# The middle stage of a two-layer transformer kernel as a wave of four batches, with another form of the scan

## The chip, the cores and the metric

The kernel runs on one core of a Trainium2 chip. The core has a matrix engine (PE, TensorE; its weight loads are counted apart as PEld), three engines for element-wise work (DVE or VectorE, ACT or ScalarE, POOL or GpSimd) and a queue for transfers (SP, SyncE). Each runs its own instructions in the order in which they are written, and they wait for each other through semaphores. The metric is the time of one execution on the device, in microseconds.

## The reference

The input is 4 x 1024 tokens of 128 features. Two layers are computed, each with an attention of 16 heads of 8 features and a second part, and each followed by a layer norm over the features (`ln` below; the norms outside have no gain or bias):

```python
# layer 0, attention part (inner residual block)
attn = causal_attention(ln(x) * g + b) @ out_w + out_b      # q, k, v by 128x128 weights
xs, vs = ln(x + attn) * g1 + b1, 0
for _ in range(8):                                            # the scan
    u  = tanh(attn @ w_ctx + xs @ w_x + b_inl)
    vs = vs + 0.1 * (u - xs - vs)
    xs = xs + 0.1 * vs
y = x + attn + xs
y = y + gelu((ln(y) * g2 + b2) @ ff_w1 + ff_b1) @ ff_w2 + ff_b2      # 128 -> 512 -> 128
x = ln(x + y)
# layer 0, second part: a linear layer plus a low-rank term
x = ln(x + x @ weight.T + pooled(x) @ disha)
# layer 1: full attention, then relu feed-forward
x = ln(x + full_attention(x) @ Wout + bout)
x = ln(x + relu(x @ W1 + b1) @ W2 + b2)
```

## The kernel before, in words

The kernel has five stages, one behind the other, each a block of its own that ends with all engines meeting: `first_stage` (norm and q, k, v of layer 0), `attention` (causal), `middle_stage`, `attention` (full), `last_stage`. Activations stay on the chip in `x_tm`, `v_tm` and `attn_tm` (tokens on partitions, 32 tiles of 128 tokens). q and k are cut into three bf16 parts, written to DRAM and loaded again per group of heads in the order that the attention wants. The attention stages follow a list of entries written out ahead (`attention_order`), with no loops left in them.

The edit is in the middle stage. It holds everything between the two attentions: the output projection of attention 0 (L889), the norm before the scan, the scan, the norm before the feed-forward, the feed-forward (L932 up, L921 down), two norms with the linear layer between them, and q, k and v of layer 1 (`Qkv`, L552 and L521).

It runs as a hardware loop of two turns (`Fori(0, NLOOP)`). One turn takes 2048 tokens as four chunks of 512; each chunk has one or two of the eight PSUM banks. On every engine the order is step by step: all four chunks of one step, then all four of the next. Features lie on partitions in most steps, so data are turned between steps by PE against an identity matrix (`turn`, L514).

The scan keeps two tensors, `xs` and a scaled velocity `w`, and the product in PSUM is never formed anew: at its start the bank gets the context term and the x term (L899, L900), and each further step adds `wx_step` times `w` (L908), which is what the change of `xs` contributes. A step of one chunk is: ACT's tanh from PSUM (L802), POOL's `u - xs` (L761), DVE's new `w` (L850), PE's addition (L908), and DVE's new `xs` (L853):

```python
pool.tensor_tensor((t if k else w)[:, c, :], u[:, c, :], xs[:, c, :], ALU.subtract)
dve.scalar_tensor_tensor(out=w, in0=w, scalar=1.0 - DT, in1=t, op0=ALU.mult, op1=ALU.add)
dve.scalar_tensor_tensor(out=xs, in0=w, scalar=DT * DT, in1=xs, op0=ALU.mult, op1=ALU.add)
pe.matmul(bank[c], wx_step, w[:, c, :], start=False, stop=True)
```

`Norm` makes statistics per tile on DVE (L472, L477), the inverse root on POOL (L504, L507: an addition and a power over the four columns of a chunk), and applies it on DVE (L484). POOL also makes the residual with a bias (L751, L766). `Qkv` brings q and k out of PSUM into fp32 with a bias (L566), makes the first bf16 part on ACT (L573), the rest on DVE for q and on POOL for k (L585), the second part on ACT (L578), and the third on DVE or POOL (L589); SP writes each chunk (L604, 384 KB a transfer) and loads the first three groups of heads for the next attention ahead. The attention's own SP program waits for the writes of all chunks.

Ahead of the stage stands a small block on DVE that scales `w_x` once (L1200) and adds the two linear weights (L1202).

Of the kernel before, what the change touches and what calls it, by code (L numbers as in the profile page):

```python
# [4 lines left out]
F32 = mybir.dt.float32  # L5
# [5 lines left out]
P = 128  # L11
# [4 lines left out]
DT = 0.1  # L16
# [26 lines left out]
FREE = 1  # L43

# [122 lines left out]
def attention(nc, taken, name, causal, scr, scr_m, slots, loaded, written, v_tm, attn_tm, ident, mask2, id2, ident_bf):  # L167
# [27 lines left out]
    with ExitStack() as ctx:  # L195
# [29 lines left out]
        def _(sp):  # L225
# [10 lines left out]
            for c in range(NCH):  # L236
                sp.wait_ge(written[c], 2 * 16 * NLOOP + FREE)
# [457 lines left out]
def middle_stage(nc, taken, W, C, R, scr, slots, loaded, written, x_tm, v_tm, attn_tm, ident, roots,  # L695
                 wx_step, w_lin):


    with ExitStack() as ctx:
        def sb(n, shape=(P, NCH, CH), dt=F32):  # L700
            return ctx.enter_context(nc.sbuf_tensor(f"m_{n}", list(shape), dt))
# [3 lines left out]


        pool3 = ctx.enter_context(nc.sbuf_tensor("m_n_x2_xx", [P, 3, NCH, CH], F32))
        n_tm = pool3[:, 0, :, :]
        x2 = y2p = pool3[:, 1, :, :]
        xx = pool3[:, 2, :, :]  # L710
        parts = pool3[:, :, :, :].rearrange("p a c t -> p (a c t)").bitcast(BF16)
        parts = parts.rearrange("p (s c j t) -> p s c j t", s=2, c=NCH, j=PARTS)
        part = [parts[:, s, :, :, :] for s in range(2)]
        both = ctx.enter_context(nc.sbuf_tensor("m_u_t", [P, 2, NCH, CH], F32))
        at = u = both[:, 0, :, :]
        aT = t = both[:, 1, :, :]
        hh = [both[:, i, :, :] for i in range(2)]
        cT = hT = sb("cT_hT")
        x1 = x3 = sb("x1_x3")
        xs = y1 = sb("xs_y1")  # L720
        w = y2 = sb("w_y2")
        bank = banks(ctx.enter_context(nc.psum_tensor("m_ps", [P, 8 * BANK], F32)))
        ln1, ln2, ln3, ln4 = (Norm(ctx, nc, taken, f"m_ln{i}", roots) for i in range(1, 5))
        qkv = Qkv(ctx, nc, taken, "m_qkv", W("q1"), W("k1"), W("v1"), C("bq1"), C("bk1"), R("bv1"),
                  scr, slots, loaded, written, v_tm, (hh[0], hh[1]), part)
        (at_ready, at_turned, aT_ready, c_mm, cT_ready, c_turned, x1_ready, n1_turned, xs_ready, z_ready,
         tanhed, lagged, sped, moved, xs_turned, xb_ready, x2_ready, xx_ready, n2_turned, hT_ready, f_mm, gelued,
         o_mm, x3_ready, y1_turned, y1T_ready, lin_mm, y2p_ready, y2_turned, y2T_ready, y2_kept) = (sem(n) for n in (
             "at_ready at_turned aT_ready c_mm cT_ready c_turned x1_ready n1_turned xs_ready z_ready tanhed lagged "
             "sped moved xs_turned xb_ready x2_ready xx_ready n2_turned hT_ready f_mm gelued o_mm x3_ready y1_turned "  # L730
             "y1T_ready lin_mm y2p_ready y2_turned y2T_ready y2_kept").split())
        block = ctx.enter_context(nc.Block())

        @block.sync
        def _(sp):
            qkv.on_sync(sp)

        @block.gpsimd
        def _(pool):
            pool.sem_inc(qkv.parted[1], FREE)  # L740
            with pool.Fori(0, NLOOP) as it:
                n0 = NCH * it
                for c in range(NCH):
                    ln1.root(pool, n0 + c, c)

                for c in range(NCH):

                    for i in range(NCH):
                        if c == 0:
                            pool.wait_ge(written[i], FREE + 2 * 16 * it)  # L750
                    pool.tensor_tensor(rows(xx[:, c, :]), x_tm[:, chunk_tiles(it, c), :],  # L751
                                       R("fb2").unsqueeze(1).to_broadcast([P, CT, P]), ALU.add)\
                        .then_inc(xb_ready, 1)
                for k in range(ITERS):
                    for c in range(NCH):
                        m = (ITERS * it + k) * NCH + c
                        pool.wait_ge(tanhed, m + 1)
                        if k:

                            pool.wait_ge(moved, m - NCH + 1)  # L760
                        pool.tensor_tensor((t if k else w)[:, c, :], u[:, c, :], xs[:, c, :], ALU.subtract)\  # L761
                            .then_inc(lagged, 1)
                for c in range(NCH):
                    pool.wait_ge(x2_ready, n0 + c + 1)
                    pool.wait_ge(xb_ready, n0 + c + 1)
                    pool.tensor_tensor(xx[:, c, :], xx[:, c, :], x2[:, c, :], ALU.add).then_inc(xx_ready, 1)  # L766
                for c in range(NCH):
                    ln2.root(pool, n0 + c, c)
                for c in range(NCH):
                    ln3.root(pool, n0 + c, c)  # L770
                for c in range(NCH):
                    ln4.root(pool, n0 + c, c)
                qkv.rest(pool, 1, it)
# [488 lines left out]
```

## Time and profile before

| | |
|---|---|
| median of 3 runs | 1732.08 us (1728.84 to 1732.10) |
| profiled execution | 1729.09 us |
| its span, from the first to the last instruction | 1727.2 us |
| PE, PEld busy | 1436.7 us (83%), 588.4 us (34%) |
| DVE busy | 1345.7 us (78%) |
| ACT busy | 1074.1 us (62%) |
| POOL busy | 403.6 us (23%) |
| mean granted TensorE clock | 0.900 of full |
| moved by DMA | 47.82 MB |

An engine is busy while one of its instructions runs; waits are not counted. Matmuls overlap, so the busy time of PE says that it had work, not how well it was used. The granted clock is a mean over a stretch in parts of the full 2.4 GHz; at any instant it is one of two levels. A matmul of fp32 data shows as two records. In order of time the first stage ends near 88 us, the first attention near 538, the middle stage near 933 and the second attention before the last stage.

### The profile page before, as it was taken

What the parts mean: (1) busy time and instruction counts of PE and PEld (TensorE: products, weight loads), DVE (VectorE), ACT (ScalarE), POOL (GpSimd) and SP (SyncE); (2) the same over time, 40 slices, a digit from 0 to 9 for tenths busy, and PEclk for the clock granted to TensorE, in tenths of its full rate; (3) what the DMA queues carried; (4) which work ended last, traced back from release to release, by engine and by line L of the source; (5) the groups of instructions that cost most, each with busy time, mean ns of one, the idle gap of its engine ahead of it and who ended that gap; (6) DMA issues with size and microseconds to landing.
All of it is one profiled execution on the core that took longest, in us unless ns stands there. A gap on an engine that the chain in (4) does not pass through costs nothing. (4 is left out here: it accounts for less than half of the span.)

```text
span 1727.2 us, 33152 instructions
## 1 busy us (share of the span) xinstructions
PE 1436.7 (83%) x13008; PEld 588.4 (34%) x13008; DVE 1345.7 (78%) x1923; ACT 1074.1 (62%) x1287; POOL 403.6 (23%) x674
## 2 busy tenths in 40 slices
PE   3379999999996667567674899999999999999767
PEld 2234344333433225431351232323333323333455
DVE  3688888888872793649656999999999999996363
ACT  3527777777775323432323588888888888888422
POOL 1512232222321762356423000000000000000331
PEclk9659999999998768776686799999999999999888
DMA  3510110101000000030002000000110000000000
GB/s 102 165 57 21 40 40 22 41 22 40 22 3 2 0 0 1 10 119 0 0 0 73 20 21 21 21 21 21 28 31 22 21 21 21 3 2 3 1 25 24
DMA packets 45456, 47.82 MB, mean 28 GB/s; under 512 B 11392, under 2 KB 32768, under 8 KB 45184
## 3 DMA queue, kind: packets, MB, share of 16 engines
q1 hardware_dynamic: 44880, 45.32, 9.0%
q8 instruction: 97, 1.59, 0.4%
q10 hardware_dynamic: 432, 0.53, 0.1%
q14 instruction: 47, 0.39, 0.1%
HBM read 30.22 MB, written 15.47 MB: 26 GB/s over the span
## 5 line engine op out<-in xcount | busy, mean ns | idle before, releaser
L338 DVE TENSOR_REDUCE l_negp<-l_ps 128x2 f32<-128x1024 f32 (+2 forms) x832 | 951.9, 1180 | 74.1 <-PE l_ps L394 35.7
L308 ACT ACTIVATE l_pT<-l_ps 128x1024 f32<-128x1024 f32 (+1 forms) x832 | 819.8, 992 | 200.3 <-PE l_ps L410 171.3
L431 PE MATMUL l_ps<-l_pT,l_vs 128*32 128x256 f32 (+3 forms) x6640 | 512.3, 384 | 2.1 <-POOL l_pT L275 1.5
L388 PE MATMUL l_ps<-Ks,Qs 48*128 48x512 bf16 (+3 forms) x1792 | 335.0, 374 | 67.6 <-DVE l_negp L338 23.9
L410 PE MATMUL l_ps<-Qs,Ks 51*128 51x512 bf16 (+3 forms) x1792 | 319.7, 365 | 15.5 <-DVE l_negp L338 8.8
L431 PEld LDWEIGHTS l_ps<-l_pT,l_vs 128*32 128x32 f32 x6640 | 134.4, 108 | 167.6 <-issue 137.9
L410 PEld LDWEIGHTS l_ps<-Qs,Ks 51*128 51x128 bf16 x1792 | 81.2, 93 | 315.8 <-issue 148.0
L388 PEld LDWEIGHTS l_ps<-Ks,Qs 48*128 48x128 bf16 x1792 | 88.4, 94 | 227.5 <-ACT l_pT L308 91.3
L275 POOL TENSOR_SCALAR_AFFINE_SELECT l_pT<-l_pT 128x512 f32<-128x512 f32 x128 | 81.1, 635 | 302.4 <-ACT l_pT L308 302.4
L908 PE MATMUL m_ps<-m_w_y,wx_step 128*128 128x512 f32 x112 | 88.8, 915 | 35.8 <-DVE m_w_y L850 35.8
L262 POOL CAST l_parts<-l_negm 128x16 bf16<-128x16 f32 x64 | 12.6, 196 | 430.5 <-DVE l_negm L343 427.4
L802 ACT ACTIVATE m_u_t<-m_ps,c_sb 128x512 f32<-128x512 f32 x64 | 44.0, 687 | 97.1 <-PE m_ps L908 85.8
L761 POOL TENSOR_TENSOR m_u_t<-m_u_t,m_xs_y 128x512 f32<-128x512 f32 x56 | 88.8, 1600 | 35.5 <-ACT m_u_t L802 20.1
L853 DVE SCALAR_TENSOR_TENSOR m_xs_y<-m_w_y,m_xs_y 128x512 f32<-128x512 f32 x64 | 75.8, 1185 | 22.0 <-POOL m_w_y L761 20.0
L394 PE MATMUL l_ps<-mask,id 64*128 64x128 bf16 x1024 | 69.6, 224 | 0.0
L850 DVE SCALAR_TENSOR_TENSOR m_w_y<-m_w_y,m_u_t 128x512 f32<-128x512 f32 x56 | 62.8, 1121 | 0.0
L322 ACT ACTIVATE l_msp<-l_ps 48x128 bf16<-48x128 bf16 x64 | 17.3, 270 | 71.0 <-PE l_ps L441 70.9
L351 DVE RECIPROCAL l_rc<-l_ps 128x16 f32<-128x16 f32 x64 | 16.5, 257 | 56.5 <-PE l_ps L448 56.5
L253 POOL COPY l_vs<-v_tm 128x256 f32<-128x256 f32 x32 | 12.7, 397 | 198.9 <-PE l_ps L431 198.8
L908 PEld LDWEIGHTS m_ps<-m_w_y,wx_step 128*128 128x128 f32 x112 | 25.1, 265 | 97.7 <-DVE m_w_y L850 91.6
L394 PEld LDWEIGHTS l_ps<-mask,id 64*128 64x128 bf16 x1024 | 50.6, 99 | 21.0 <-issue 2.3
L514 PE MATMUL m_ps<-ident,m_n_x_xx 128*128 128x128 f32 x64 | 17.8, 434 | 40.5 <-DVE m_n_x_xx L484 40.5
(139 smaller groups left out, 1241.6 us busy)
## 6 DMA issues: line engine op xcount, KB each, us to landing
Qs<-scr_q SPq DMA_DIRECT2D x128, 64.0 KB
Ks<-scr_k SPq DMA_DIRECT2D x64, 96.0 KB
Qs<-scr_q SPq DMA_DIRECT2D x128, 32.0 KB
Ks<-scr_k SPq DMA_DIRECT2D x64, 64.0 KB
scr_q<-a_part SPq DMA_DIRECT2D x8, 384.0 KB, 3.7
scr_k<-a_part SPq DMA_DIRECT2D x8, 384.0 KB, 3.9
scr_q<-m_n_x_xx SPq DMA_DIRECT2D x8, 384.0 KB, 4.2
scr_k<-m_n_x_xx SPq DMA_DIRECT2D x8, 384.0 KB, 4.2
```

Of the source, the lines that this page charges most:

```text
L275: pool.affine_select(out=blk, in_=blk, compare_op=ALU.is_ge, fill=0.0, base=0, pattern=[[0, GH], [1, P]], channel_multiplier=-1).then_inc( ...
L308: act.activation(dst, src, ACT.Exp, scale=SCALE).then_inc(exped, 1)
L338: dve.tensor_reduce(dst, src, AX_X, ALU.max, negate=True).then_inc(reduced, 1)
L388: last = pe.matmul(outs[par], Qs[s][r:r + MROW, h2, qt * P:(qt + 1) * P], Ks[s][r:r + MROW, h2, at:at + w], start=True, stop=True)
L394: last = pe.matmul(outs[par][:, w - P:w], id2[r:r + ROWS, j, :], mask2[r:r + ROWS, j, :], start=False, stop=True, skip_group_check=True)
L410: last = pe.matmul(to[:, par, i * w:(i + 1) * w], Ks[s][r:r + MROW + 3, h2, kt * P:(kt + 1) * P], Qs[s][r:r + MROW + 3, h2, qh * CH + lo:( ...
L431: last = pe.matmul(pv_ps[q % 2][32 * h:32 * h + 32, a:a + wide], vs[g % 2][:, kt, h, :], pT[m % PRING][:, h, a:a + wide], start=n == first ...
L761: pool.tensor_tensor((t if k else w)[:, c, :], u[:, c, :], xs[:, c, :], ALU.subtract)\
L802: act.activation(u[:, c, :], bank[c], ACT.Tanh, bias=C("b_inl")).then_inc(tanhed, 1)
L850: dve.scalar_tensor_tensor(out=w[:, c, :], in0=w[:, c, :], scalar=1.0 - DT, in1=t[:, c, :], op0=ALU.mult, op1=ALU.add).then_inc(sped, 1)
L853: dve.scalar_tensor_tensor(out=xs[:, c, :], in0=w[:, c, :], scalar=DT * DT, in1=xs[:, c, :], op0=ALU.mult, op1=ALU.add).then_inc(moved, 1)
L908: pe.matmul(bank[c], wx_step, w[:, c, :], start=False, stop=True, skip_group_check=True)\
```

## The change

The signatures carry `written_all`, so that the attention waits for as much as the stage before it wrote. The middle stage is rewritten without a loop. Its unit is a batch of 1024 tokens with two PSUM banks of its own from the first step to the last, and all engines walk through one list, in which batch b is five steps behind batch b - 1:

```diff
+def wave(steps, lag):
+    order = [(i + lag * b, b, name) for i, name in enumerate(steps) for b in range(B)]
+    return [(name, b) for _, b, name in sorted(order)]
...
+    steps = (["turn_attn", "out", "turn_out", "scale1", "turn1", "ctx"] + [("scan", k) for k in range(ITERS)]
+             + ["turn_xs", "scale2", "turn2"] + [("up", j) for j in range(4)] + [("down", i) for i in range(4)]
+             + ["scale3", "turn3", "lin", "scale4", "turn4", "q", "k", "v"])
+    order = wave(steps, LAG)
```

One entry of the list is one step of one batch: a name that each engine looks up for its own share. `batch_mm` is two matmuls of 512 columns, `turn_batch` eight transposes, `batch_tokens_out` eight matmuls of 128 columns; `RowNorm` does statistics, root and scaling for eight tiles at once.

The scan keeps `x` alone, at two neighbouring steps in a ring of two buffers. Velocity is eliminated: x(k+1) is a combination of x(k), x(k-1) and the tanh, and a factor `BETA`, the root of 1 - 0.1, per step makes the coefficient of x(k-1) minus one. The factors go into scaled copies of `w_x`, one per step. In each step the context term is multiplied anew, and then the x term is added to it:

```diff
+                elif name[0] == "scan":
+                    k = name[1]
+                    now, then = ring[b][k % 2], ring[b][(k + 1) % 2]
+                    dve.wait_ge(tanhed[b % 2], ITERS * (b // 2) + k + 1)
+                    dve.wait_ge(lagged[b % 2], ITERS * (b // 2) + k + 1)
+                    dve.scalar_tensor_tensor(out=then, in0=u[b], scalar=DT * DT / BETA ** (k + 1), in1=then,
+                                             op0=ALU.mult, op1=ALU.add).then_inc(moved[b % 2], 1)
+                    if k < ITERS - 1:
+                        dve.wait_ge(moved[b % 2], ITERS * (b // 2) + k + 1)
+                        dve.scalar_tensor_tensor(out=now, in0=then, scalar=(2.0 - DT - DT * DT) / BETA, in1=now,
+                                                 op0=ALU.mult, op1=ALU.subtract).then_inc(lagged[b % 2], 1)
...
+                elif name[0] == "scan":
+                    k = name[1]
+                    if k:
+                        pe.wait_ge(tanhed[b % 2], ITERS * (b // 2) + k)
+                        batch_mm(pe, bank[b], W("ctx"), cT[b])
+                        pe.wait_ge(moved[b % 2], ITERS * (b // 2) + k)
+                    batch_mm(pe, bank[b], wx_of[k], ring[b][k % 2], start=False).then_inc(z_ready[b % 2], 1)
```

Further: the transposes of the attention's output read `attn_tm` itself; the identity is added to the linear weight, so that the residual comes out of the matmul and the fourth norm reads PSUM (`ln4.stats(dve, b, bank[b])`) and writes `x_tm` directly; POOL does only the two residual adds and the roots; the feed-forward's four hidden tensors lie in the scan's ring, `x1` and the norm's buffer; q and k go from PSUM straight to their first bf16 part on ACT, the rest and the third part on DVE. Gelu of one batch and tanh of later ones share ticks of the order. SP writes each batch in two transfers and waits for them before the stage ends:

```diff
+            for name, b in order:
+                if name == "v":
+                    for s in range(2):
+                        sp.wait_ge(s_parted[s], b + 1)
+                        dst = scr[s][:, :, b * SEQ:(b + 1) * SEQ]
+                        sp.dma_start(dst.rearrange("(j d) h t -> (d h) j t", d=HD), parts[:, b, s, :, :])\
+                            .then_inc(written[b], 16)
+                    if b == 0:
+                        sp.wait_ge(written[0], 32)
+                        for g in range(NG - 1):
+                            load_group(sp, scr, slots, loaded, g)
+            for b in range(B):
+                sp.wait_ge(written[b], 32)
...
+                for k in range(1, ITERS):
+                    dve.tensor_scalar(wx[:, k - 1, :], W("x"), BETA ** k, None, ALU.mult)
+                dve.tensor_tensor(w_lin[:, :], W("lin"), W("dis"), ALU.add).then_inc(lin_added, 1)
+                dve.wait_ge(lin_added, 1)
+                dve.tensor_tensor(w_lin[:, :], w_lin[:, :], ident[:, :], ALU.add)
```

## Rows read from the trace of the kernel before

**Rows 1.** The page: span, and busy time of the engines.
```profile
span 1727.2 us, 33152 instructions
PE 1436.7 (83%) x13008; PEld 588.4 (34%) x13008; DVE 1345.7 (78%) x1923; ACT 1074.1 (62%) x1287; POOL 403.6 (23%) x674
```

**Rows 2.** Order of time at the stage's ends: start us, us, engine line op, idle before.
```profile
541.23 0.23 DVE L1200 TENSOR_SCALAR wx_step<-w_sb 128x128 f32<-128x128 f32 x1 [3.00 <-PEq L115]
...
932.25 1.13 SPq L604 DMA_DIRECT2D scr_k<-m_n_x_xx  x1
...
933.83 0.61 PE L388 MATMUL l_ps<-Ks,Qs 48*128 48x512 bf16 x2 [15.71 <-PEq L699]
```

**Rows 3.** Busy us of PE, PEld, DVE, ACT, POOL (and count) by stretch; clock, DMA share, GB/s.
```profile
538.00:571.00 33.00, 14.99 (x59) 10.46 (x60) 15.78 (x55) 11.59 (x17) 9.77 (x12) 0.70 0.00 1
571.00:638.00 67.00, 49.26 (x69) 14.85 (x68) 59.55 (x52) 21.21 (x31) 47.87 (x30) 0.73 0.00 0
660.00:694.00 34.00, 30.57 (x165) 21.32 (x163) 8.74 (x39) 13.42 (x19) 3.09 (x6) 0.95 0.00 1
694.00:734.30 40.30, 23.88 (x108) 17.15 (x108) 25.70 (x78) 20.73 (x36) 14.70 (x17) 0.76 0.03 10
734.30:931.00 196.70, 130.54 (x432) 70.51 (x432) 128.15 (x280) 69.81 (x106) 92.47 (x83) 0.73 0.11 33
```

**Rows 4.** Who waited for whom in the middle stage: us in total, times, longest.
```profile
PEld m_ps L908 <- DVE m_w_y L850: 91.6, 48, 3.1
ACT m_u_t L802 <- PE m_ps L908: 85.8, 56, 3.6
```

**Rows 5.** Order of time in the scan, DVE and POOL.
```profile
628.94 0.68 DVE L850 SCALAR_TENSOR_TENSOR m_w_y<-m_w_y,m_u_t 128x512 f32<-128x512 f32 x1
629.03 5.05 POOL L761 TENSOR_TENSOR m_u_t<-m_u_t,m_xs_y 128x512 f32<-128x512 f32 x3 [0.56 <-DVE m_xs_y L853]
...
631.21 1.75 DVE L850 SCALAR_TENSOR_TENSOR m_w_y<-m_w_y,m_u_t 128x512 f32<-128x512 f32 x1
```

**Rows 6.** Order of time on PE, four stretches without a wait inside.
```profile
544.59 3.41 PE L514 MATMUL m_ps<-ident,m_u_t 128*128 128x128 f32 x16 [6.97 <-ACT m_u_t L784]
...
551.27 1.91 PE L514 MATMUL m_ps<-ident,m_cT_hT 128*128 128x128 f32 x16
...
668.59 3.73 PE L921 MATMUL m_ps<-w_sb,m_u_t 128*128 128x128 f32 x32
...
672.16 3.60 PE L932 MATMUL m_ps<-m_cT_hT,w_sb 128*128 128x512 f32 x8
```

**Rows 7.** ACT: order of time at the first gelu; then L308, ns min/median/max.
```profile
660.06 0.78 ACT L805 ACTIVATE m_cT_hT<-m_ps,c_sb 128x512 f32<-128x512 f32 x1 [0.51 <-PE m_ps L514]
...
660.85 1.28 ACT L813 ACT_TABLE_LOAD   x1
...
662.15 0.69 ACT L813 ACTIVATE m_u_t<-m_ps,c_sb 128x512 f32<-128x512 f32 x1
...
L308 ACT ACTIVATE l_pT<-l_ps x832: 592/1023/1138, 114.2 to 1604.9; 128x1024 f32<-128x1024 f32 x151, 128x512 f32<-128x512 f32 x16
```

**Rows 8.** Order of time in the norms; then L338, ns min/median/max.
```profile
556.55 0.36 DVE L477 BATCH_NORM_AGGREGATE m_ln_mv<-m_ln_bst 128x2 f32<-128x6 f32 x4
...
557.27 1.01 POOL L507 TENSOR_TENSOR m_ln_rs<-m_ln_ve,neg_half 128x4 f32<-128x4 f32 x1
...
646.19 0.87 DVE L472 BATCH_NORM_STATS2 m_ln_bst<-m_n_x_xx 128x6 f32<-128x128 f32 x4
646.23 1.26 POOL L766 TENSOR_TENSOR m_n_x_xx<-m_n_x_xx 128x512 f32<-128x512 f32 x1 [4.62 <-DVE m_n_x_xx L857]
...
653.61 1.11 DVE L484 TENSOR_SCALAR m_n_x_xx<-m_n_x_xx,m_ln_mv,m_ln_rs 128x128 f32<-128x128 f32 x4 [1.52 <-POOL m_ln_rs L507]
...
L338 DVE TENSOR_REDUCE l_negp<-l_ps x832: 679/1218/1228, 89.5 to 1580.3; 128x2 f32<-128x1024 f32 x135, 128x4 f32<-128x512 f32 x16, 128x2 f32<-128x768 f32 x16
```

**Rows 9.** L604, the writes of q and k: issue to landing.
```profile
DMA to landing us min/median/max: 2.5/4.1/6.2
```

More of the change, by code:

```diff
@@ L43 @@
 FREE = 1
+LAG = 5
 def part_runs(order):
@@ new lines, in turn_batch, with batch_mm, batch_tokens_out @@
+def turn_batch(pe, bank, src, ident):
+    for t in range(QT):
+        last = pe.transpose(bank[:, t * P:(t + 1) * P], src[:, t * P:(t + 1) * P], ident)
+    return last
+def batch_mm(pe, bank, weight, src, start=True):
+    for i in range(QH):
+        last = pe.matmul(bank[:, i * CH:(i + 1) * CH], weight, src[:, i * CH:(i + 1) * CH], start=start, stop=True,
+                         skip_group_check=not start)
+    return last
+def batch_tokens_out(pe, bank, src, weight):
+    for t in range(QT):
+        last = pe.matmul(bank[:, t * P:(t + 1) * P], src[:, t * P:(t + 1) * P], weight, start=True, stop=True)
+    return last
@@ L712, in middle_stage @@
[L712 to L731, printed above, removed]
+        three = sb("three", (P, B, 3, SEQ))
@@ L732, in middle_stage @@
+        f_mm, gelued = sem("f_mm"), sem("gelued")
+        assert LAG >= 4 and 2 * LAG >= ITERS
+        z_ready, tanhed, moved, lagged = (
+            [sem(f"{n}{i}") for i in range(2)] for n in "z_ready tanhed moved lagged".split())
+        s_mm, s_first, s_rest, s_second, s_parted = (
+            [sem(f"{s}_{n}") for s in "qk"] for n in "mm first rest second parted".split())
         block = ctx.enter_context(nc.Block())
@@ L738, in _ @@
+            for b in range(B):
+                sp.wait_ge(written[b], 32)
         @block.gpsimd
         def _(pool):
[L740 to L773, printed above, removed]
@@ new lines, in _ @@
+            for name, b in order:
+                if name == "turn_attn":
+                    pool.tensor_tensor(rows(xx[b]), rows(xs_tm[b]), R("fb2").unsqueeze(1).to_broadcast([P, QT, P]),
+                                       ALU.add).then_inc(xb_ready, 1)
+                elif name == "turn_out":
+                    ln1.root(pool, b)
+                elif name == "turn_xs":
+                    ln2.root(pool, b)
+                    pool.wait_ge(x2_ready, b + 1)
+                    pool.wait_ge(xb_ready, b + 1)
+                    pool.tensor_tensor(xx[b], xx[b], x1[b], ALU.add).then_inc(xx_ready, 1)
+                elif name == ("down", 3):
+                    ln3.root(pool, b)
+                elif name == "lin":
+                    ln4.root(pool, b)
```

371 lines of the change are left out of this document (204 added, 167 removed).

## The prediction

> **What bounds the kernel now.** I read the page, then busy time by stretch, then the waits of the middle stage, then the order of time inside it. The page gives 1727.2 us of span in an execution of 1729.09 us [rows 1]; the shown median, 1732.08, lies 3.0 above. The edit rewrites only the middle stage, and the two attention stages, the first and the last stage keep their work. So the question is what lies between 541.23, where the small block of weights ahead of the stage begins, and 933.83, the first matmul of the second attention [rows 2]: 392.6 us.
>
> In that stretch no engine is full. The second of the two like loop turns is 196.7 us long with PE busy 130.5, DVE 128.2, ACT 69.8, POOL 92.5, at a granted clock of 0.73 [rows 3], a mix of TensorE's two levels, 1.2 and 2.4 GHz. It is a chain with little beside it. In the scan (571 to 638) DVE is busy 59.6 of 67 us and PE 49.3, at 0.73; in the up and down matmuls (660 to 694) PE is busy 30.6 of 34 at 0.95; in layer norm, linear and QKV (694 to 734) PE 23.9 of 40.3 at 0.76. The waits agree: of the stage's waits, PE's weight loads wait 91.6 us for DVE's `w`, ACT's tanh 85.8 us for PE [rows 4]. And DVE is full there only because POOL is: a scalar_tensor_tensor of 512 columns takes 0.69 us while POOL rests and 1.75 us while POOL subtracts [rows 5]. The stage ends on waits, and a denser order can win time.
>
> **Cost of the pieces, for 1024 tokens.** PE, at full clock: eight records of L932 (four 512-column matmuls) take 3.60 us, so a pair takes 1.71; 32 records (16 small matmuls) of L921 3.73, so eight take 1.86; 16 transposes 1.91 (3.41 at the low level), so eight take 0.92 [rows 6]. ACT: 0.59 us at 512 columns and 1.02 at 1024 without a bias, 0.69 with a bias at 512; so 1.12 with a bias, 1.21 with a scale too [rows 7]. DVE: 0.68 us at 512 columns and 1.22 at 1024 [rows 8], so 1.22 for an add, as a lone scan operation's 0.68 [rows 5] agrees with at 512, and two dependent operations of the scan 2.4; statistics (0.87 and 0.36 for four tiles, issued closer than they last) 2.3 for eight; a scale 2.1 (1.11 for four); POOL's root, 1.01 for four columns and not shown for eight, between 1.0 and 2.0: I take 2.0, since the addition beside it costs 0.2 on as many columns and so the cost sits in the power itself; with the addition and gaps 2.5 [rows 8].
>
> **What goes and what comes.** Gone: 64 POOL subtractions, half of DVE's columns under contention, the copy of attention into `at`, eight x_tm copies, the adds before the fourth norm. The scan keeps two scalar_tensor_tensor a step, and the first alone stands before the next matmul; POOL is idle in it, so I price them uncontended. POOL's eight adds of 1024 columns (about 2.5 us each from 1.26 at 512 [rows 8]) can hold DVE for up to 1.1 us each at the contended price; at DVE's 186 us in some 300 that is covered, and uncovered it is 8 x 1.1 = 9 us. Added: per step and batch another ctx matmul. Before, the scan had 8 x 9 = 72 matmuls of 512 columns; now it has 4 x 8 x 4 = 128: 56 x 0.855 = 48 us more PE work at full clock. PE's sum per batch: 23 pairs (39.3), six groups of eight small ones (11.2) and seven groups of eight transposes (6.4), so 57 and 228 us for four. DVE's is 15 scan operations at 1.2 (18.0), three adds with statistics (10.5), lin's statistics (2.3), four scales (8.9), the start of the scan (0.7, between half and all of 1.2), q, k and v (6.0): 46.4, so 186.
>
> **The order.** 33 steps a batch, five apart, make 48 ticks. Within a tick I take the largest of PE's sum, DVE's sum and the longest single step. PE by step: transposes 0.92; out, ctx, the first scan step, each up, q and k 1.71; the other seven scan steps 3.42; each down, lin and v 1.86; the scales none. Single steps: a scan step is tanh 1.12, two pairs 3.42 (the ctx pair covers DVE's 1.22) and gaps, 4.8; the first 4.2; turn_out and turn_xs 6.9; the last down 7.9; lin 6.7; up 3.0; q and k 4.4; scales 2.3 (the fourth, which reads PSUM and which no row shows, 2.8, my estimate, bounds 2.3 and 3.3); v 3.3; other transposes 2.2 to 2.4; out 3.0. The ticks:
> 0 to 9: 2.2 3.0 6.9 2.3 2.4 2.6 4.2 6.9 4.8 4.8, together 40.1;
> 10 to 29: 6.0 6.8 8.3 6.8 6.9 6.0 7.8 9.5 8.6 7.0 6.8 7.9 10.4 10.4 9.4 6.6 7.1 8.8 7.0 7.9, together 156.2 (PE's own sum 148.5);
> 30 to 47: 5.4 5.4 7.3 3.6 7.9 4.4 4.5 6.7 2.8 7.9 4.4 4.4 6.7 2.8 2.2 4.4 4.4 3.3, together 88.5.
> Tick 22, as an example, holds down 1 of batch 0, up 0 of batch 1 and a scan step of batches 2 and 3: 1.86 + 1.71 + 3.42 + 3.42 = 10.4 on PE, beside 4.8 of DVE. Sum 284.8.
>
> At 148 of 156 us PE is as dense as in 660 to 694, so the full clock holds there. In ticks 33 to 47 PE has 40.5 of 70 us, the share of 694 to 734; at that clock, 0.76, it adds 40.5 x 0.316 = 13; the first five, 4.5 us of PE at the 0.70 of 538 to 571 [rows 3], add 2. That makes 300 us.
>
> ACT changes function set wherever a gelu and a tanh share a tick: 17 to 20, 22 to 25, 27 and 28, two loads each, and one at 29: 21 loads of 1.28 us [rows 7], 27 us on ACT. Its worst tick becomes 3.4 + 2.6 = 6.0 beside 9.5 of PE: covered. In the trace the load begins 0.01 us behind the activation before it ends and the gelu starts 1.30 after the load began [rows 7]; I price a switch at 1.3.
>
> The Trainium skill (ScalarE: Activation LUTs, "What ACT_TABLE_LOAD costs") gives a switch some 2.66 us, load and drain, and tells authors to do all calls of one set together, which this wave undoes. By it the 21 switches are 56 us; the trace does not show the drain.
>
> **Both ends of the stage.** Ahead: seven more small operations on DVE at 0.23 [rows 2], the dependent add, then a barrier: 3.0 us from 541.23. Behind: SP now waits for each batch's writes inside the stage. Landing took 4.1 us in the median and 6.2 at most for 384 KB [rows 9], now 768 KB; the last `v` (3.3) covers part: 5 us, bounds 0 and 10. Unrolling puts loops' code into a straight line; I price that at nothing, as the attention's is such.
>
> Sum: 1729.1 - 392.6 + 3.0 + 300 + 5 = 1644.5; at the median's level 1647.
>
> **Rivals.**
> (a) Queues hold each other: every engine runs strictly in the written order, so each of 16 scales that waits 2.5 us for POOL's root holds the scan operations queued behind it on DVE. If all show on PE: 16 x 2.5 = 40 us, 1687. For: DVE's sum passes PE's in ticks 12, 14, 24. Against: a whole tick of other batches' work lies between statistics and scale.
> (b) The function sets end on the path: gelu holds the tanh of the scan. 27 us: 1674; for it, ticks 19, 20, 24, 25 have one or two scans and little cover; against it ACT's low share. At the skill's price it would be 1703.
> (c) Slower: PE becomes the bound at the low clock. The new stage rests on PE; the scan before ran at 0.73. With PE's terms divided by the clock the ticks give 354 us at 0.73 (1701), 389 at 0.65, and 490 at the lowest level throughout (1837). It turns slower below about 0.66. For: 32 batch steps with waits in them. Against: the dense ticks look like 660 to 694.
> (d) Better packing: chains of neighbouring ticks overlap, which my maximum per tick forbids. Ticks 0 to 9 of batch 0 alone (40), PE's 148, and the last batch's steps from tick 30 (58) give 246, some 50 less: 1593 at the very best; a third of it is 1628.
> That the change does not thin the scan's DVE work would show as (a).
>
> **Chances.** Forecast 0.58, (a) 0.15, (b) 0.08, (c) 0.08, three parts in four of it slower, (d) 0.11. The range is 1618 to 1692: it leaves out most of (c) and the far ends of (a) and (d). A difference of 0.2% is about what can be told from none here. Faster 0.93, same 0.01, slower 0.06.
>
> **What would show it.** PE over 85% busy at a clock above 0.9 in ticks 16 to 24; scan operations on DVE near 1.2 us, not 1.7; 21 or so table loads; the stage about 308 us from the weights block to the attention's first matmul. PE waits for DVE of more than 40 us in all would show (a), waits for gelu and tanh (b), a clock under 0.8 (c). Any change in the attention stages' time would make the sum wrong.

## The result, and the profile after

| | before | after |
|---|---|---|
| median | 1731.24 us (1728.84 to 1732.10, four executions) | 1658.05 us (1655.79 to 1660.02, four executions) |
| ratio, with its 95% interval | | 0.9579 [0.9561, 0.9597] |
| profiled execution, span | 1729.09, 1727.2 us | 1656.61, 1654.9 us |
| mean granted clock | 0.900 | 0.935 |

The change is faster by 73 us; the forecast had 84 (1647), and the range held it. The page of the kernel after answers to [rows 1]: POOL's busy time falls by 123 us, DVE's by 55 and ACT's by 41, while that of PE, the busiest, hardly moves (1436.7 to 1432.2): the span falls because PE waits less. PE has more matmuls than before and runs them at a higher clock.

```profile
span 1654.9 us, 32470 instructions
PE 1432.2 (87%) x13120; PEld 596.0 (36%) x13120; DVE 1290.7 (78%) x1850; ACT 1032.7 (62%) x1164; POOL 280.6 (17%) x554
```

The order of time at the ends of the middle stage, kernel after (start us, us, engine, line, operation, idle before), answers to [rows 2]:

```profile
542.72 1.04 DVE L1268 TENSOR_SCALAR wx<-w_sb 128x128 f32<-128x128 f32 x7 [3.00 <-PEq L116]
544.59 1.94 PE L742 MATMUL m_ps<-ident,attn_tm 128*128 128x128 f32 x8 [5.49 <-PEq L1261]
...
858.01 1.22 DVE L947 TENSOR_TENSOR v_tm<-m_ps,r_sb 128x1024 f32<-128x1024 f32 x1 [1.19 <-PE m_ps L757]
861.69 0.61 PE L389 MATMUL l_ps<-Ks,Qs 48*128 48x512 bf16 x2 [3.72 <-PEq L776]
```

From 542.72 to 861.69 are 319.0 us, against 392.6 before and 308 in the forecast. What lies behind the stage is unchanged (1654.9 - 861.69 = 793.2, before 1727.2 - 933.83 = 793.4); what lies ahead is 1.5 us longer. So the profiled execution is 12.1 above the forecast's 1644.5, of which 11.0 are in the stage: ahead 1.9 us (forecast 3.0), the ticks from 544.59 to the last `v` at 859.23 314.6 (forecast 300), behind 2.5 (forecast 5).

Busy us of PE, PEld, DVE, ACT, POOL (and count) by stretch, then clock, DMA share and GB/s, kernel after. The stretches are the whole stage, then the ticks 0 to 9, 10 to 29 and 30 to 47 with the end; they answer to [rows 3]:

```profile
542.70:862.00 319.30, 254.01 (x978) 147.99 (x980) 201.26 (x491) 97.63 (x89) 57.85 (x41) 0.89 0.08 28
542.70:595.60 52.90, 30.78 (x88) 16.12 (x89) 26.09 (x68) 9.94 (x9) 12.54 (x7) 0.73 0.00 1
595.60:763.60 168.00, 155.01 (x542) 84.09 (x541) 113.80 (x237) 57.60 (x52) 29.76 (x18) 0.96 0.00 0
763.60:861.70 98.10, 67.91 (x352) 47.66 (x351) 61.27 (x186) 30.09 (x29) 15.25 (x16) 0.86 0.25 89
```

In the dense middle PE is busy 155 of 168 us at a clock of 0.96. Measured against the forecast, ticks 0 to 9 took 51.0 us (42.1 with the clock's 2), 10 to 29 168.0 (156.2), 30 to 47 95.6 (101.5 with the clock's 13).

Who waited for whom in the stage (us in total, times, longest), kernel after, answers to [rows 4]. `PE` is the matmul itself, `PEld` the load of its weights:

```profile
ACT m_three L863 <- PE m_ps L749: 80.2, 32, 4.3
PE m_ps L742 <- DVE m_three L734: 27.4, 8, 9.9
PE m_ps L742 <- DVE x_tm L734: 11.0, 3, 7.2
...
PEld m_ps L749 <- DVE m_three L905: 6.2, 5, 2.6
...
PE m_ps L749 <- DVE m_three L905: 2.6, 3, 1.8
```

The same two waits in the kernel before, for the scan's `w`:

```profile
PEld m_ps L908 <- DVE m_w_y L850: 91.6, 48, 3.1
PE m_ps L908 <- DVE m_w_y L850: 35.8, 35, 2.3
```

PE hardly waits for the scan any more: the weight loads 6.2 us for its x (L905) instead of 91.6, the matmuls 2.6 instead of 35.8. Tanh still waits 80 us for PE, as it must where PE is the bound. What stands out now is the second row: the transposes (L742) wait for a norm's scale (L734). The groups of the stage, kernel after (busy us, mean ns of one, idle before and what ended it), say what the scan's operations on DVE and the scale cost:

```profile
L905 DVE SCALAR_TENSOR_TENSOR m_three<-m_three 128x1024 f32<-128x1024 f32 x32 | 39.0, 1218 | 58.8 <-ACT m_three L863 58.7
L734 DVE TENSOR_SCALAR m_three<-attn_tm,m_ln_mv,m_ln_rs 128x128 f32<-128x128 f32 x96 | 39.9, 488 | 7.5 <-POOL m_ln_rs L729 7.5
L729 POOL TENSOR_TENSOR m_ln_rs<-m_ln_ve,neg_half 128x8 f32<-128x8 f32 x16 | 30.3, 1892 | 1.3
```

A scan operation takes 1.22 us for 1024 columns, against 1.75 for 512 beside POOL in [rows 5]. But one scale of 128 columns takes 488 ns in the mean, and the twelve groups of eight, 39.9 us in all, are 14 us above twelve times the 2.14 us that eight take alone. The order of time, kernel after, shows why:

```profile
558.58 1.65 POOL L729 TENSOR_TENSOR m_ln_rs<-m_ln_ve,neg_half 128x8 f32<-128x8 f32 x1
560.20 2.34 POOL L832 TENSOR_TENSOR v_tm<-x_tm,r_sb 128x1024 f32<-128x1024 f32 x1
560.27 4.15 DVE L734 TENSOR_SCALAR m_three<-attn_tm,m_ln_mv,m_ln_rs 128x128 f32<-128x128 f32 x8 [2.05 <-POOL m_ln_rs L729]
...
628.09 2.14 DVE L734 TENSOR_SCALAR m_three<-attn_tm,m_ln_mv,m_ln_rs 128x128 f32<-128x128 f32 x8
634.97 2.61 POOL L729 TENSOR_TENSOR m_ln_rs<-m_ln_ve,neg_half 128x8 f32<-128x8 f32 x1
637.55 2.35 POOL L840 TENSOR_TENSOR v_tm<-v_tm,attn_tm 128x1024 f32<-128x1024 f32 x1
637.62 6.20 DVE L734 TENSOR_SCALAR m_three<-attn_tm,m_ln_mv,m_ln_rs 128x128 f32<-128x128 f32 x8 [1.53 <-POOL m_ln_rs L729]
639.86 2.34 POOL L832 TENSOR_TENSOR v_tm<-x_tm,r_sb 128x1024 f32<-128x1024 f32 x1
...
643.88 1.97 PE L742 MATMUL m_ps<-ident,m_three 128*128 128x128 f32 x8 [4.42 <-DVE m_three L734]
```

and, with two scales in a row,

```profile
729.75 6.33 DVE L734 TENSOR_SCALAR m_three<-attn_tm,m_ln_mv,m_ln_rs 128x128 f32<-128x128 f32 x16
...
731.30 2.39 POOL L840 TENSOR_TENSOR v_tm<-v_tm,attn_tm 128x1024 f32<-128x1024 f32 x1
```

One event, the end of POOL's root, releases two things at once: DVE's scale, and POOL's next instruction, which is the residual add of 1024 columns. The add begins 0.07 us ahead of the scale, and the scale lasts longer by most of the add: 4.15 instead of 2.14 with one add, 6.20 with two (L840 and then L832). At 643.88 PE has waited 4.4 us for it, with nothing else to do in the written order, and starts again with eight transposes at the low level (1.97 us; [rows 6] has 1.91 for sixteen). Seven of the eight adds lie on a scale: four begin 0.06 or 0.07 us ahead of it, one follows straight behind another add, and two (731.30 and 770.26) begin 1.6 and 0.9 us behind the start of two scales in a row. The loss is the same there: sixteen scales take 6.33 us, against 4.28 for two groups alone.

The Trainium skill (SBUF — State Buffer, "Who interferes with whom") has a rule that bears on this: it names tensor_scalar among the operations that can enter a mode with two ports and then contend with GpSimd, and says that whoever issues first holds the shared pair for the whole instruction. The trace agrees where the add comes first: 0.07 us behind it, the scale loses 2.0 us.

### The profile page after: what moved, and what is told of

Read it like the earlier page. It is cut to its first block and busy times, and to the rows that moved or that the text cites. A ratio compares the mean times of both kernels' runs of the same rounds, so it can differ in the third digit from the quotient of the medians.

```text
span 1654.9 us, 32470 instructions
## 1 busy us (share of the span) xinstructions
PE 1432.2 (87%) x13120; PEld 596.0 (36%) x13120; DVE 1290.7 (78%) x1850; ACT 1032.7 (62%) x1164; POOL 280.6 (17%) x554
## 3 DMA queue, kind: packets, MB, share of 16 engines
q8 instruction: 101, 1.65, 0.4%
## 5 line engine op out<-in xcount | busy, mean ns | idle before, releaser
L749 PE MATMUL m_ps<-m_cT_hT,w_sb 128*128 128x512 f32 x224 | 113.2, 639 | 12.7 <-DVE attn_tm L937 8.7
L863 ACT ACTIVATE m_three<-m_ps,c_sb 128x1024 f32<-128x1024 f32 x32 | 35.7, 1115 | 80.2 <-PE m_ps L749 80.2
L905 DVE SCALAR_TENSOR_TENSOR m_three<-m_three 128x1024 f32<-128x1024 f32 x32 | 39.0, 1218 | 58.8 <-ACT m_three L863 58.7
L749 PEld LDWEIGHTS m_ps<-m_cT_hT,w_sb 128*128 128x128 f32 x224 | 42.7, 203 | 60.1 <-issue 40.6
L749 PE MATMUL m_ps<-m_three,wx 128*128 128x512 f32 x112 | 53.2, 597 | 2.6 <-DVE m_three L905 2.6
L727 POOL TENSOR_TENSOR m_ln_ve<-m_ln_mv,eps 128x8 f32<-128x8 f32 x16 | 8.7, 546 | 232.7 <-DVE m_ln_mv L722 232.7
L1110 DVE TENSOR_TENSOR e_x<-e_ps,e_yb 128x512 f32<-128x512 f32 x8 | 5.5, 692 | 52.0 <-PE e_ps L1140 41.0
```

Of the source, the lines that this page charges most:

```text
L749: last = pe.matmul(bank[:, i * CH:(i + 1) * CH], weight, src[:, i * CH:(i + 1) * CH], start=start, stop=True, skip_group_check=not start)
L863: act.activation(u[b], bank[b], ACT.Tanh, bias=C("b_inl")).then_inc(tanhed[b % 2], 1)
L905: dve.scalar_tensor_tensor(out=then, in0=u[b], scalar=DT * DT / BETA ** (k + 1), in1=then, op0=ALU.mult, op1=ALU.add).then_inc(moved[b % 2 ...
```

## Experiments

All were timed beside the kernel before, which read 1730.2 to 1731.2 us each time; ratios are to it, with 95% intervals. "After" is the changed kernel at 1658.05. The theory: the wave does what the forecast says, PE is the bound in its middle, and the missing 11 us are POOL's adds on DVE's scales. The rivals: the root itself holds the queues (a), the function sets (b), the low clock (c), or the rule for the ticks is wrong.

### POOL's eight adds made small

Each add covers 8 columns instead of 1024, so the residual is left out of most columns.

```diff
-                    pool.tensor_tensor(rows(xx[b]), rows(xs_tm[b]), R("fb2").unsqueeze(1).to_broadcast([P, QT, P]), ALU.add).then_inc(xb_ready, 1)
+                    pool.tensor_tensor(xx[b][:, 0:8], xs_tm[b][:, 0:8], R("fb2")[:, 0:8], ALU.add).then_inc(xb_ready, 1)
...
-                    pool.tensor_tensor(xx[b], xx[b], x1[b], ALU.add).then_inc(xx_ready, 1)
+                    pool.tensor_tensor(xx[b][:, 0:8], xx[b][:, 0:8], x1[b][:, 0:8], ALU.add).then_inc(xx_ready, 1)
```

> Leaves out most of POOL's eight residual adds in the middle stage: each works on 8 of 1024 columns, so the stage's results are not the reference's. All waits stay. Theory A (POOL's adds hold DVE while it scales, and PE waits for the scaled tile): the scales fall from 4.2 and 6.2 us to 2.1 each, PE's waits for them (27.4 us in the new kernel) fall to about 15, and the time falls by 10 to 15 us, to about 1645. Theory B (what PE waits for is the root and the written order of the queues, not the adds): the waits stay and the time falls by less than 4 us, to 1655 or more.

1639.88 us, ratio 0.9471 [0.9455, 0.9487]: 18.2 less than after, more than the 10 to 15 expected. Of PE's wait of 27.4 us for the scales,

```profile
PE m_ps L742 <- DVE m_three L734: 14.2, 6, 7.8
```

is left. The roots and the order of the queues are as they were, so these 18 us were not rival (a) in its own form, every scale waiting for its root; they were the adds.

### The adds at other places

First only the four with the bias, all made at the start of the stage, ahead of every root; then the other four as well, on DVE behind the second scale.

```diff
+            for b in range(B):
+                pool.tensor_tensor(rows(xx[b]), rows(xs_tm[b]), R("fb2").unsqueeze(1).to_broadcast([P, QT, P]), ALU.add).then_inc(xb_ready, 1)
             for name, b in order:
-                if name == "turn_attn":
-                    pool.tensor_tensor(rows(xx[b]), rows(xs_tm[b]), R("fb2").unsqueeze(1).to_broadcast([P, QT, P]), ALU.add).then_inc(xb_ready, 1)
```

The other four, in the second kernel beside these:

```diff
-                    pool.tensor_tensor(xx[b], xx[b], x1[b], ALU.add).then_inc(xx_ready, 1)
...
                     ln2.scale(dve, b, x1[b], n_tm[b])
+                    dve.wait_ge(xb_ready, b + 1)
+                    dve.tensor_tensor(xx[b], xx[b], x1[b], ALU.add).then_inc(xx_ready, 1)
```

> POOL makes the four bias adds at the start of the stage, where DVE has nothing to do, and no longer behind a root of another batch; the other four adds stay. Theory A: half of the locks go. The scale at 560 us and the one at 590 us last 2.1 us and not 4.2, the one at 638 us 4.2 and not 6.2; 5 to 8 us less, about 1651. Theory B: 0 to 2 us less.

> As the kernel with the four bias adds first, and the other four adds are done by DVE itself behind the second scale (1.2 us each) and not by POOL (2.35 us) beside it. Theory A: no lock is left; close to the kernel in which the adds are nearly left out, 2 us above it at most, about 1646. Theory B: the same as the kernel after or up to 5 us slower, since DVE has 5 us more to do.

1648.76 us (0.9524 [0.9508, 0.9540]), 9.3 less than after where 5 to 8 were expected, and 1639.63 (0.9472 [0.9456, 0.9487]), 18.4 less. The second keeps the whole computation and gets as much as leaving the adds out. In the first, the scales that the expectation names last 2.14, 2.14 and 4.16 us, as expected. The second kernel's group of the same scales, and the same scale as at 637.62 in the kernel after:

```profile
L734 DVE TENSOR_SCALAR m_three<-attn_tm,m_ln_mv,m_ln_rs 128x128 f32<-128x128 f32 x96 | 25.5, 343 | 7.5 <-POOL m_ln_rs L729 7.5
```

```profile
634.72 2.14 DVE L734 TENSOR_SCALAR m_three<-attn_tm,m_ln_mv,m_ln_rs 128x128 f32<-128x128 f32 x8 [1.53 <-POOL m_ln_rs L729]
```

The group is 14.4 us shorter (39.9 - 25.5), and the stage 17.3 (319.0 to 301.7, from 542.85 to 844.58), so in sum the holds were on the path, and something came on top. DVE does four more adds of 1024 columns than in the kernel after, and nothing is lost by it. Ticks 10 to 29 of this kernel, in the columns of [rows 3]:

```profile
593.06:748.59 155.53, 150.22 (x541) 80.83 (x541) 108.69 (x240) 57.65 (x52) 20.50 (x14) 0.99 0.00 1
```

They take 155.5 us instead of 168.0. Of these 12.5 us, 7.7 are PE's idle time (13.0 to 5.3) and 4.8 its busy time, which falls from 155.0 to 150.2 for the same matmuls as the granted clock rises from 0.96 to 0.99. So a held scale costs twice: PE waits for it, and after the wait runs its next pieces at the low level, as at 643.88.

### The context term not multiplied anew

The step's product keeps the old PSUM content out: `wx` times x alone from the second step on, so the context term is left out of seven of eight steps.

```diff
-                        pe.wait_ge(tanhed[b % 2], ITERS * (b // 2) + k)
-                        batch_mm(pe, bank[b], W("ctx"), cT[b])
                         pe.wait_ge(moved[b % 2], ITERS * (b // 2) + k)
-                    batch_mm(pe, bank[b], wx_of[k], ring[b][k % 2], start=False).then_inc(z_ready[b % 2], 1)
+                    batch_mm(pe, bank[b], wx_of[k], ring[b][k % 2], start=k > 0).then_inc(z_ready[b % 2], 1)
```

> Leaves the repeated context product out of scan steps 1 to 7 (the x term alone starts the bank), so the stage's results are not the reference's; 56 matmuls of 512 columns and 48 us of PE work at full clock go. If PE is the bound in ticks 10 to 29, as the prediction has it, its sum there falls from 148 to about 105, DVE's 110 and the chains take over, and the time falls by 30 to 40 us, to about 1622. Rival: the chain through tanh and DVE sets the end and PE's product is hidden beside it, then less than 10 us go.

1628.81 us, 0.9407 [0.9392, 0.9423]: 29.2 less than after. That is just below what was expected, 30 to 40 us. The rule for the ticks with these 28 pairs (28 x 1.71 = 48 us of PE) taken out gives 27 us, but this was worked out afterwards. Most of the rest of the 48 turns into waits, since the pair no longer covers DVE's update. PE's wait for the scan's x, 2.6 us in the kernel after, is here

```profile
PE m_ps L749 <- DVE m_three L905: 15.9, 7, 4.0
```

### The wave with the old scan, and the old loop with the new scan

One half of the change each: the wave, in which POOL, DVE and PE do the scan as before, and the loop of before, in which they do it as after.

```diff
+                elif name[0] == "scan":
...
+                    pool.tensor_tensor(u[b] if k else ring[b][1], u[b], ring[b][0], ALU.subtract)\
+                        .then_inc(lagged[b % 2], 1)
...
+                        dve.scalar_tensor_tensor(out=ring[b][1], in0=ring[b][1], scalar=1.0 - DT, in1=u[b],
+                                                 op0=ALU.mult, op1=ALU.add).then_inc(sped[b % 2], 1)
...
-                        batch_mm(pe, bank[b], W("ctx"), cT[b])
```

and, against the kernel before,

```diff
-                        pool.tensor_tensor((t if k else w)[:, c, :], u[:, c, :], xs[:, c, :], ALU.subtract)\
-                            .then_inc(lagged, 1)
...
+                        dve.scalar_tensor_tensor(out=then[:, c, :], in0=u[:, c, :], scalar=DT * DT / BETA ** (k + 1),
+                                                 in1=then[:, c, :], op0=ALU.mult, op1=ALU.add).then_inc(moved, 1)
...
+                        pe.matmul(bank[c], W("ctx"), cT[:, c, :], start=True, stop=True)
```

> The wave of four batches with the scan of before: position and velocity, POOL's subtraction, the context product only once. It does one part of the change alone. With the tick rule of the prediction: PE's step falls to 1.71 us, but POOL's subtraction of 1024 columns (2.35 us) and DVE's two operations (2.4) exclude each other, so a batch's step costs that pair 4.8 us and the chain 6.8; the sum of the ticks is 317 instead of 285, so the time is about 1658 + 32 = 1690. Rival: the wave is the whole gain and the form of the scan does not matter, then the time is 1658 or less, since PE has 48 us less to do.

> The kernel of before, its loop over chunks of 512 kept, with the new scan alone: x only, context term anew in each step. It does the other part alone. A step of four chunks is then eight matmuls of 512 columns, 6.9 us at full clock, beside 5.3 us of DVE without POOL's locks; 8 steps are 56 us against 72 before, two turns: 32 us less, about 1700. Rival: the clock stays at the 0.73 of the old scan, then a step is 9.4 us and nothing is won, 1731 or more.

The wave with the old scan takes 1714.47 us, 0.9902 [0.9885, 0.9918], 16 less than before and 24 above what was expected. The loop with the new scan takes 1694.65, 0.9789 [0.9773, 0.9806], 36 less. Apart they bring 52 us, together 73. The waits of the first and its order of time show what was underrated:

```profile
DVE m_three L905 <- POOL m_three L841: 99.4, 21, 6.6
PE m_ps L749 <- DVE m_three L905: 70.0, 19, 10.7
```

```profile
663.38 2.34 POOL L847 TENSOR_TENSOR v_tm<-v_tm,attn_tm 128x1024 f32<-128x1024 f32 x1
665.67 2.34 POOL L841 TENSOR_TENSOR m_three<-m_three 128x1024 f32<-128x1024 f32 x1
668.04 1.22 DVE L905 SCALAR_TENSOR_TENSOR m_three<-m_three 128x1024 f32<-128x1024 f32 x1 [6.63 <-POOL m_three L841]
```

POOL's subtraction stands in each step's chain at 2.34 us, and here it queued behind one of POOL's other adds; the batches share one queue. The wave is worth more once POOL is out of the scan. How much of the 24 us comes from the queue, and how much from a PE with less to do and a lower clock (0.911), no run shows. In the loop, the same stretch as in [rows 3] (571 to 638: PE 49.26 of 67 us, clock 0.73) now reads

```profile
571.00:638.00 67.00, 59.01 (x148) 27.04 (x146) 49.38 (x93) 22.78 (x33) 6.71 (x8) 0.93 0.00 0
```

PE is busy 88% of the stretch instead of 74% and is granted 0.93, for all its extra context products. The scan is also over sooner: its last operation on DVE starts at 628.80, and the old scan is still running at 640. So with the new scan 8.5 of the 67 us already belong to the norm behind it.

### Exponential in place of tanh

The kernel after has one table load in the stage, not 21: at 655.64, ahead of the first gelu (L872), and none at a tanh behind it. To see 21 switches, the scan's function was replaced by another, so its results are not the reference's.

```diff
-                    act.activation(u[b], bank[b], ACT.Tanh, bias=C("b_inl")).then_inc(tanhed[b % 2], 1)
+                    act.activation(u[b], bank[b], ACT.Exp, bias=C("b_inl"), scale=0.01).then_inc(tanhed[b % 2], 1)
```

> The kernel after with exp in the place of tanh in the scan (scale 0.01), so the results are not the reference's. The trace of the kernel after shows one table load at the first gelu and none at a tanh behind a gelu, so tanh lies in gelu's set and the 21 switches of the prediction never came. Before the attention's first exp there is a load, so exp is in another set: this kernel has them. The prediction's step (21 loads of 1.28 us are covered by PE): 1658 to 1661. Rival of the prediction (b): all on the path, 1685; at 2.66 us a switch 1714.

1659.03 us, 0.9578 [0.9562, 0.9594]: 1.0 above after, within what can be told from none. Its groups count 21 loads, and the order of time shows one of them:

```profile
L872 ACT ACT_TABLE_LOAD x11 | 14.1, 1283 | 0.2
L863 ACT ACT_TABLE_LOAD x10 | 12.8, 1283 | 0.6 <-DVE m_three L905 0.4
```

```profile
656.19 1.11 ACT L854 ACTIVATE m_cT_hT<-m_ps,c_sb 128x1024 f32<-128x1024 f32 x1 [0.60 <-PE m_ps L749]
657.32 1.28 ACT L872 ACT_TABLE_LOAD   x1
658.61 1.11 ACT L872 ACTIVATE m_three<-m_ps,c_sb 128x1024 f32<-128x1024 f32 x1
```

27 us of loads lie beside PE, as the forecast had it. A switch is 658.61 - 657.30 = 1.31 us from the end of one activation to the start of the next, load and gap. The Trainium skill (ScalarE: Activation LUTs, "What ACT_TABLE_LOAD costs") gives 2.66 us with the drain. The load agrees; the drain is not in this trace, and 1.31 us is what counts here.

### Idle matmuls at the ends

21 more matmuls whose results nobody reads, 8 behind the third step of batch 0 and 13 in the last steps of batch 3.

```diff
+                    if b == 0:
+                        for _ in range(8):
+                            pe.matmul(bank[3][:, 0:CH], W("x"), W("f1"), start=True, stop=True)
...
```

> The kernel after with 21 further matmuls of 512 fp32 columns whose product nobody reads, put where PE waits for a norm or for q and k: 8 behind the first batch's third step, 8 behind the last lin, 1 and 2 and 2 behind it. They can only hold the clock up. If the low clock at both ends costs what the prediction has (15 us), part of it comes back: the last transposes, q, k and v take 1.0, 1.9, 1.9 and 1.9 us instead of 2.0, 3.8, 3.8 and 3.5, and 6 to 8 us go, about 1651. Rival: the clock does not matter where chains set the end, 1658 or, by the added work, up to 5 us more.

1654.03 us, 0.9553 [0.9537, 0.9569]: 4.0 less than after, below the 6 to 8 that were expected. The low clock of the ends costs some us; it is not the main term.

### Batches four or six steps apart

```diff
-LAG = 5
+LAG = 4
```

> The kernel after with the batches four steps apart instead of five: 45 ticks instead of 48. The prediction's tick rule (largest of PE's sum, DVE's sum and the longest step) gives 285.0 us of ticks against 284.8: fuller ticks, fewer of them, so the same time, 1655 to 1661. Rival: the ends, where one batch is alone, are what costs, and three ticks fewer take 10 us off, 1648.

> The kernel after with six steps between batches: 51 ticks. The tick rule gives 295.0 us against 284.8, so about 1668. Rival: waits inside a tick (the order of the queues) are what the kernel loses, and more distance takes them away: 1658 or less.

Six apart: 1668.10 us, 0.9646 [0.9630, 0.9662], 10.0 above after. The rule gives 10.2 (295.0 to 284.8). Four apart: 1651.83, 0.9550 [0.9534, 0.9566], 6.2 less where the rule gives 0. The scales, first four and then six apart, read

```profile
L734 DVE TENSOR_SCALAR m_three<-attn_tm,m_ln_mv,m_ln_rs 128x128 f32<-128x128 f32 x96 | 33.6, 421 | 9.7 <-POOL m_ln_rs L729 9.7
L734 DVE TENSOR_SCALAR m_three<-attn_tm,m_ln_mv,m_ln_rs 128x128 f32<-128x128 f32 x96 | 31.6, 401 | 3.6 <-POOL m_ln_rs L729 3.6
```

which is 6.3 and 8.3 us less than the 39.9 of the kernel after: with another distance some adds fall beside other work. Four apart, that is as much as the gain. Six apart, it speaks against the rule: the kernel lost 10.0 us although its scales were held 8.3 us less, so the distance by itself probably costs more than 10, and the agreement with 10.2 is in part luck. Six apart was not run with the adds moved. Four apart was, in the last kernel.

### A better kernel, and the same four steps apart

The adds moved, the idle matmuls, and k's product in the two banks of the batch before, so that it need not wait until q has left its own, and v waits for q alone. The second has LAG = 4 beside.

```diff
+        def qk_bank(s, b):
+            return bank[b - 1] if s and b else bank[b]
...
-                    batch_mm(pe, bank[b], W(f"{name}1"), yT[b]).then_inc(s_mm[s], 1)
+                    batch_mm(pe, qk_bank(s, b), W(f"{name}1"), yT[b]).then_inc(s_mm[s], 1)
...
-                    pe.wait_ge(s_rest[1], b + 1)
+                    pe.wait_ge(s_rest[0 if b else 1], b + 1)
```

> Three things together on the kernel after: the eight adds moved (the four bias adds first, the other four on DVE), the idle matmuls at both ends, and k's product into the banks of the batch before, so that k no longer waits until q's remainder is read out and v waits for q's alone. The first gave 18.4 us and the second 4.0. The third takes two waits of 2.5 us out of the last batch's chain: 4 to 5 us. If they add, 1631. Rival: v of the last batch waits for ACT and DVE anyway and only the first two count, 1636.

> The kernel with the eight adds moved, the idle matmuls and k in its neighbour's banks, and four steps between batches in the place of five. Four steps alone gave 6.2 us. If that came from shorter ends, it adds up to about 1626; if it came from POOL's adds, which fall elsewhere with another distance, it is gone here and the time is 1631 or more.

1631.87 us, 0.9429 [0.9414, 0.9445]: 26 less than after, 98 less than before, and the fastest of those that leave nothing out. The adds (18.4) and the idle matmuls (4.0) leave 3.8 us for k's product, which was not run alone. Its stage, and PE's wait for the scales:

```profile
541.00:840.00 299.00, 263.03 (x1026) 151.86 (x1026) 193.67 (x498) 97.27 (x89) 50.51 (x41) 0.93 0.09 30
```

```profile
PE m_ps L742 <- DVE m_three L734: 10.5, 6, 4.1
```

Four apart it takes 1636.87, 0.9460 [0.9441, 0.9480], 5 more in the medians (four executions from 1633.5 to 1639.5, against 1629.4 to 1632.4). So a shorter distance is worth nothing once the adds are moved, and costs some us where the rule has 0; that its gain in the kernel after came from where the adds fell is the reading that fits both. The rule is blind to something at this distance, and what it is was not looked for.

## Why the prediction was right or wrong

**The frame held.** All of the change is in the stage; 793 us behind it stood still, and the sum could be made against 392.6 us.

**PE as the bound: right.** In ticks 16 to 24 (643.9 to 724.5) PE is busy 79.1 of 80.6 us at a clock of 0.97, where the prediction wanted more than 85% and 0.9. That is against rival (c): its 0.73 came only in ticks 0 to 9. The best support for the rule of the largest sum per tick is the kernel with the adds moved, whose ticks 10 to 29 take 155.5 us for a forecast of 156.2. As a forecast of differences the rule is weaker: -27 without the context pairs, for 29 measured, was worked out afterwards (on record were 30 to 40), +10.2 six apart met 10.0 with a different share of held scales, and 0 four apart missed by 6 and, with the adds moved, by 5. The context product costs 29 us on the path, of 48 us of PE's work.

**The scan on DVE: right.** 1.22 us an operation where 1.22 was priced, and 2.6 us left of the matmuls' waits for it.

**"POOL's eight adds ... covered": the step that failed.** The forecast was 11 us too low, and this is the term that accounts for it; it was put at nothing. Three things in it were wrong. The size: an add takes 2.34 us and holds DVE for 2.0, not "up to 1.1". The partner: it was priced by the contention of the scan's two-input operations in [rows 5]; what it met was the scale, an operation with one tensor input. And the cover: DVE's total of 186 in 300 us says nothing, since the add is released by the same event as the scale and PE's next work stands behind that scale. Seven adds meet a scale, 14.4 us on DVE, and taking them away is worth 18. With the bound as written (8 x 1.1 = 9) taken as uncovered, the forecast would have been 1656; with 8 x 2.0 it would have been 1663. So part of the miss is the price, and the rest is that a scale held on the path also brings PE's low level behind it. The order of POOL's queue, root and then add, could be read from the code.

The meeting itself stands in the trace of the kernel before, outside the rows that the prediction shows. In the norm ahead of the scan, POOL's residual adds (L751) follow the last root, and DVE's scale (L484) starts 0.06 us behind the first of them:

```profile
562.90 4.92 POOL L751 TENSOR_TENSOR m_n_x_xx<-x_tm,r_sb 128x512 f32<-128x512 f32 x4
562.96 4.94 DVE L484 TENSOR_SCALAR m_n_x_xx<-m_x_x,m_ln_mv,m_ln_rs 128x128 f32<-128x128 f32 x4 [0.41 <-POOL m_ln_rs L507]
...
567.96 1.12 PE L514 MATMUL m_ps<-ident,m_n_x_xx 128*128 128x128 f32 x4 [4.23 <-DVE m_n_x_xx L484]
```

Four scales take 4.94 us there instead of the 1.11 of [rows 8], beside four adds of 512 columns, and PE waits 4.2 us behind them. So the price, about 1 us for 512 columns and 2 for 1024, the partner and the wait on PE could all have been read before the change.

**Without that term the forecast was too high.** The kernel with the adds moved has a stage of 301.7 us for the forecast's 308: its ends come to 4.3 us (1.9 and 2.4) instead of 8, and its ticks to 297.4 for 300. That much less, -6.3, and the 17.3 of the adds make the 11.0 that the stage is above the forecast. That the ticks come to within 3 us is luck in part: ticks 0 to 9 take 48.4 us there for a forecast of 42.1, ticks 10 to 29 155.5 for 156.2, and ticks 30 to 47 93.6 for 101.5, so 6 us too little at the head and 8 too much at the tail cancel.

**The clock.** In the kernel after the parts were off in both directions: the head lost more than the 2 us put in (a clock of 0.50 from 544.6 to 571 instead of 0.70; its first pair takes 3.78 us, one at 580.15 and at full clock 1.98; and two scales are held by adds), the tail probably less than 13 (0.82 instead of 0.76 in ticks 33 to 47, from 784.4 on). The idle matmuls gave back 4.0 of 15.

**Function sets: right in price, wrong in number.** One load, not 21; with 21 made, +1.0 us. Rival (b) falls either way. [rows 7], on which the number rests, show the load ahead of the first gelu and no tanh behind a gelu, so they could not say.

**Rival (a)** was near in its place, the scales of the norms, and wrong in its mechanism: with the roots as they are and the adds small, PE's wait for twelve of the sixteen scales halves. With the adds moved, DVE waits 13.8 us for roots (7.5 and 6.3 for the four scales that read PSUM), and PE 14.2 and 11.0 us for the scales, most of it in the ends, where one batch is alone: in ticks 10 to 29 2.4 us are left. The sign that the prediction named for (a), more than 40 us of PE's waits for DVE in all, did appear (27.4 + 11.0 + 8.7 + 3.0 + 2.6 + 0.6 = 53.3 us in the kernel after) without the time that goes with it, 1687: it also counts the waits of the ends and those for held scales, and so could not tell (a) from them. The root's own price, 2.0 us, lay between what it takes: 1.65, and 2.61 where a scan operation of DVE had begun 0.11 us ahead of it. It is 2.61 with the adds moved, too, so that is not the adds' doing.

**Rival (d)**, better packing, is not seen beyond the 2.6 us in the ticks.

Still open is what a held scale costs without the clock: in ticks 10 to 29 PE's busy time gives 4.8 of the 12.5 us, but no run held the clock fixed, and for the ends the split was not made.

## What to carry to other kernels

Before you call a side engine's work covered, look at what releases it: if it is next in its queue behind the same event that releases the critical engine's next operation, the two start together every time, and a share of busy time says nothing. Look for the same pair of operations in the trace that you have: it may show the price. Put such work ahead of the chain or on the engine that does the urgent operation, behind it; here this gained 18 us and kept all the work. A sum per tick, with the largest of the engines' sums taken, was good to 1 us in 156 where PE is dense and nothing holds it. In the ends, where one batch's chain sets the time, it was off by 6 to 8 us either way, and between two distances of the batches by some 5 us. A sum that comes out right can hide such errors; check it by stretch.

## What the runs showed of the hardware

- An fp32 scale (tensor_scalar, two per-partition scalars, 128 columns from and to SBUF) is held by a POOL add of 1024 columns beside it: eight take 2.14 us alone, 4.15 with one add that began 0.07 us before, 6.20 with two adds; in the kernel before, four take 4.94 beside four adds of 512 columns, and 1.11 alone; sixteen take 6.33 with one that began 1.6 us after the first.
- Tanh behind gelu needs no table load: one load in the stage after, 21 with the exponential in its place; each 1.28 us, 1.31 from the end of one activation to the start of the next.
- POOL's power over eight columns took 1.65 us beside a resting DVE, and also at 625.17, where DVE's two-input operation began 0.5 us after it; it took 2.61 where one had begun 0.11 us before it (634.97, and 632.07 with the adds moved). The add over 1024 columns took 2.34.
- Behind a wait of 4.4 us, at 643.88, PE's eight transposes take 1.97 us and the pair behind them 3.62, at the low level; the next pair takes 1.99. Behind a wait of 1.5 us, at 689.85, eight transposes take 1.09, at the high level.
